# Four-block network on one core: the last layer norms start during the last attention group, the shared expert comes before the routed ones, and the end goes in four blocks

## The chip, the cores and the metric

One core of one Trainium2 chip. The metric is the device time of the kernel in microseconds (us); lower is better.

## The reference

2048 tokens of 128 numbers pass four sub-blocks, each of the form `x = x + norm(f(norm(x)))`: linear attention, a feed-forward with low-rank experts, causal attention that keeps the 64 largest scores of a row, and a second feed-forward. Only the last one and the norms around it matter here:

```python
x = x + _layernorm(_L1_attn_ref(_layernorm(x, axis=-1), ...), axis=-1)
x = x + _layernorm(_L1_ffn_ref(_layernorm(x, axis=-1), ...), axis=-1)
...
normed = _layernorm(hidden_states, ln_w, ln_b)
xf = normed.reshape(-1, h)
logits = xf @ router_w
top_idx = jnp.argmax(logits, axis=-1)
top_score = jax.nn.sigmoid(jnp.max(logits, axis=-1))
w = jnp.where(top_idx == e, top_score, 0.0)[:, None]      # for each expert e of 8
xe = xf * w
hmid = jax.nn.silu(xe @ g) * (xe @ u)
routed = routed + hmid @ d
shared = jax.nn.silu(xf @ sh_gate) * (xf @ sh_up) @ sh_down
moe_out = (routed + shared)
return hidden_states + moe_out
```

So between the attention and the router stand three norms: that of the attention's output, that before the feed-forward, and the feed-forward's own with a weight and an offset (`ln_w`, `ln_b`). The feed-forward's input is added to its output before the last norm.

## The kernel before, in words

The 2048 tokens are 16 tiles of 128 rows; a tile lies on the 128 partitions. The third sub-block runs in 64 groups k of four heads, four groups for each tile (tile t is groups 4t to 4t+3). The scores of group k stand in slot k mod 3 of a ring `S` in the large buffer `R`; each slot has 8256 numbers a partition. `SA` and `BIG` are names of parts of `R`: `SA` starts at slot 0, `BIG` at slot 2, and behind slot 2 lie the two scratch rows `A`.

The engines work in program order and meet at semaphores. Around the last group (k = 63, NG = 64) the order of each is this:

- VectorE (`dve`): pivots, MAX8 searches and `threshold` for each group; the last thing of a group is four masks (L1263). Then `memory_weights(63)` (L1353) and `weigh_heads` of groups 62 and 63 (L1259), a wait for the last accumulation `s_acc`, and the norms over all 16 tiles: `normalize` (L1019) does 16 `bn_stats`, 16 `bn_aggr`, an addition of epsilon, waits for ScalarE's square root, a reciprocal and 16 scalings. Norm, residual into `X`, norm, norm, two affine passes over all tiles (L1374, L1375).
- ScalarE (`act`): `exponent` of the four heads (L614), the copy `drain_heads(62)` (L597), then one drain for each of the 16 turned blocks of the group (`drain_turn`, L621), `drain_rest`, `drain_heads(63)`. Only then `sqrt(6)`, `sqrt(7)`, `sqrt(8)` (L471). A change to a function of another table puts an ACT_TABLE_LOAD ahead of it.
- TensorE (`pe`): in `values(k)` for each block j a turn (L890, L891: transposition of four score blocks with the mask) into one of two PSUM banks, then the product with the values (L906). Turn j+1 is issued ahead of product j; a turn waits until the drain of the bank two turns earlier is done, product j for drain j. `outputs(63)` closes the group (L924, L927).
- GpSimd (`pool`): four additions for the heads of each group (L442 to L451) after `rden`; the last one adds to `ACC` and raises `s_acc`.
- SyncE (`sp`): reload of `X` (L370) when the last MAX8 is done (`s_eight`), then `ln_w`, `ln_b` and six weight loads (L373 to L380) when group 63 is turned, then the output as one transfer (L382).

The second feed-forward starts when the normed rows `N1` are written (`s_rows` 4). TensorE turns all four blocks of four tiles (L963), computes the router's logits for 16 tiles (L969) and waits; VectorE finds the expert (`first_max`), ScalarE makes the sigmoid, VectorE multiplies the rows by the score (L1383, `s_rows` 5), TensorE turns those (L975). Then come 36 rounds, one for each expert e and block b of 512 tokens, e = 0 to 7 routed and e = 8 (`E0`) shared: `up(n)` makes gate and up (L986), ScalarE applies silu to the gate (L670), VectorE multiplies (`hidden`, L1397), `down(n)` (L994), and VectorE adds into `Y` (`gather`, L1411 for a routed expert, L1407 for the shared one). `plan_ffn1` lists the PSUM fills in order with the engine that drains each; fill n goes into bank n mod 8 after fill n-8 is drained. The up of round n+1 is issued ahead of the down of round n:

```python
up(0)
for n in range(4 * (E0 + 1)):
    if n + 1 < 4 * (E0 + 1):
        up(n + 1)
    down(n)
```

After the last round VectorE norms all 16 tiles, adds to `X` (L1425), and SyncE writes the 1 MB.

## Time and profile before

| | us |
|---|---|
| median of 3 runs (2819.96 to 2825.53) | 2820.38 |
| profiled execution, its own time | 2827.31 |
| span of the profiled execution | 2825.4 |
| TensorE matmuls busy in it | 2227.3 (79%) |
| VectorE busy in it | 2221.3 (79%) |
| ScalarE busy in it | 1570.8 (56%) |
| GpSimd busy in it | 563.0 (20%) |

The span is the time between the first and the last thing recorded on the core; its own time has 1.9 us around it. Shares of busy time are means over stages of very different kind. In the rows, PE is TensorE, DVE VectorE, ACT ScalarE, POOL GpSimd and SP SyncE; an engine's name with a q is its instruction queue, L with a number a line of the kernel, and a bracket at the end of a row gives the idle time before it and what ended that. Granted clock 1.00 is 2.4 GHz and 0.50 is 1.2 GHz; a value between them is a stretch with both.

### The profile page before, as it was taken

To read this page: it belongs to the slowest core of one execution; us is meant where nothing else is said; L and a number is where in the kernel's file an instruction comes from. 1 tells how busy PE (TensorE), PEld (TensorE's weight loads), DVE (VectorE), ACT (ScalarE), POOL (GpSimd) and SP (SyncE) were. 2 spreads that over 40 slices of the span, in tenths; PEclk is the share of its full clock that TensorE was granted. 3 is DMA by queue.
4 is the path that set the end of the run, shared out by engine and by line. 5 is a ranking of instruction groups with operands and counts; after the bars stand their busy time and mean duration, and the time that the engine had idled before them with its cause. 6 is when DMAs were issued, how large, how long until landed. Compare 5 with 4: busy or idle time off the path is not lost.

```text
span 2825.4 us, 34844 instructions
## 1 busy us (share of the span) xinstructions
PE 2227.3 (79%) x10182; PEld 1302.3 (46%) x10182; DVE 2221.3 (79%) x8987; ACT 1570.8 (56%) x2335; POOL 563.0 (20%) x427
## 2 busy tenths in 40 slices
PE   6599546677787668888888888898957888973997
PEld 2555333334444334455444445455434444542664
DVE  2504599999999989999999999888888878755445
ACT  1121234555666557777777777777737767661221
POOL 0000012222223222232222223223111312320000
PEclk7699667778989889999999999999978999986999
DMA  2000000000000000000000000000000000001000
GB/s 64 1 1 1 15 1 1 1 1 1 1 1 1 0 1 1 1 1 1 1 1 1 1 1 1 1 1 1 1 0 1 1 1 1 1 16 53 1 1 15
DMA packets 18021, 13.65 MB, mean 5 GB/s; under 512 B 6924, under 2 KB 15766, under 8 KB 17814
## 3 DMA queue, kind: packets, MB, share of 16 engines
q1 hardware_dynamic: 13776, 8.92, 1.2%
q10 hardware_dynamic: 4038, 2.37, 0.3%
q8 instruction: 81, 1.33, 0.2%
q14 instruction: 126, 1.03, 0.1%
HBM read 9.19 MB, written 2.10 MB: 4 GB/s over the span
## 4 chain that ended last, share of the span: by engine, by line
PE 45%; DVE 30%; ACT 17%; issue 6%; DVEq 2%; ACTq 1%; POOL 0%; POOLq 0%
PE bank L906 11%; PE bank L874 9%; DVE cand L1190 8%; ACT signs L591 5%; PE bank L890 5%; PE bank L986 4%; ACT R L614 3%; ACT R L564 3%; DVE W L1222 3%; DVE W L1221 3%; PE bank L891 3%; ACT R L607 2%; DVE F L1263 2%; PE bank L994 2%; PE bank L790 1%
## 5 line engine op out<-in xcount | busy, mean ns | idle before, releaser
L906 PE MATMUL bank<-WP,Y 128*128 128x512 f32 x1088 | 645.6, 679 | 168.0 <-ACT WP L621 166.2
L874 PE MATMUL bank<-hT,qT 128*128 128x512 f32 (+3 forms) x1280 | 564.9, 578 | 144.2 <-ACT R L564 96.2
L1190 DVE MAX8 cand<-R 128x8 f32<-128x12 f32 (+15 forms) x4096 | 666.9, 221 | 7.9 <-ACT R L564 7.4
L431 POOL TENSOR_TENSOR X<-R,X 128x144 f32<-128x144 f32 (+15 forms) x64 | 164.3, 2568 | 1934.0 <-ACT X L607 1934.0
L621 ACT ACTIVATE WP<-bank 128x512 f32<-128x512 f32 x544 | 320.9, 593 | 259.3 <-PE bank L891 249.0
L890 PE MATMUL bank<-ident,R 128*128 128x128 f32 x2176 | 446.2, 288 | 14.9 <-ACT R L614 14.9
L874 PEld LDWEIGHTS bank<-hT,qT 128*128 128x128 f32 x1280 | 237.7, 205 | 392.4 <-issue 185.9
L891 PE MATMUL bank<-nidentb,F 128*128 128x128 bf16 x2176 | 416.0, 226 | 0.0
L890 PEld LDWEIGHTS bank<-ident,R 128*128 128x128 f32 x2176 | 320.2, 147 | 154.6 <-issue 110.6
L564 ACT ACTIVATE R<-bank 128x1024 f32<-128x1024 f32 (+7 forms) x384 | 290.3, 773 | 156.5 <-PE bank L874 92.7
L614 ACT ACTIVATE R<-R,negm 128x144 f32<-128x144 f32 (+15 forms) x256 | 309.9, 1213 | 100.3 <-DVEq L1347 100.3
L591 ACT ACTIVATE signs<-R,cutb 128x144 int8<-128x144 f32 (+15 forms) x256 | 309.1, 1207 | 1.6
L891 PEld LDWEIGHTS bank<-nidentb,F 128*128 128x128 bf16 x2176 | 230.5, 106 | 132.5 <-issue 132.5
L906 PEld LDWEIGHTS bank<-WP,Y 128*128 128x128 f32 x1088 | 178.0, 206 | 227.1 <-ACT WP L621 220.5
L1263 DVE TENSOR_SCALAR F<-R,thr 128x144 bf16<-128x144 f32 (+15 forms) x256 | 197.0, 771 | 78.8 <-PE bank L891 77.3
L1250 DVE SCALAR_TENSOR_TENSOR R<-R,r 128x144 f32<-128x144 f32 (+15 forms) x128 | 235.7, 1841 | 4.5
L431 POOL TENSOR_TENSOR R<-R 128x144 f32<-128x144 f32 (+15 forms) x64 | 228.3, 3567 | 0.0
L1222 DVE TENSOR_TENSOR W<-W 128x256 f16<-128x256 f16 x768 | 216.8, 282 | 0.0
L1221 DVE TENSOR_TENSOR W<-W 128x256 f16<-128x256 f16 x768 | 207.9, 271 | 0.4
L1252 DVE MAX8 r<-R 128x8 f32<-128x144 f32 (+15 forms) x128 | 167.9, 1311 | 4.4
L607 ACT ACTIVATE X<-R,cutb 128x144 f32<-128x144 f32 (+15 forms) x64 | 77.5, 1212 | 137.6 <-DVE cutb L1236 137.6
L670 ACT ACTIVATE R<-bank 128x512 f32<-128x512 f32 x76 | 45.4, 597 | 146.6 <-PE bank L986 138.3
(239 smaller groups left out, 2720.3 us busy)
## 6 DMA issues: line engine op xcount, KB each, us to landing
out<-X SPq DMA_DIRECT2D x2, 1024.0 KB, 5.1
R<-in_L_attn_Wkv ACTq DMA_DIRECT2D x2, 512.0 KB, 8.4
R<-in_L_ffn_gate_w SPq DMA_DIRECT2D x1, 1024.0 KB, 6.4
R<-in_L_ffn_up_w SPq DMA_DIRECT2D x1, 1024.0 KB, 9.4
R<-in_L_attn_Wq ACTq DMA_DIRECT2D x1, 512.0 KB, 6.5
WP<-in_L_attn_Wo ACTq DMA_DIRECT2D x1, 512.0 KB, 11.1
R<-in_L_ffn_wi SPq DMA_DIRECT2D x1, 256.0 KB
R<-in_L_ffn_wo SPq DMA_DIRECT2D x1, 256.0 KB
```

Source lines behind the costliest of these rows:

```text
L431: pool.tensor_tensor(OV[i - 2][:, 0:n], S[:, k % NS, i, 0:n], OV[i - 2][:, 0:n], ALU.subtract)\
L564: act.activation(S[:, k % NS, i, MEM + SC * c:MEM + SC * c + w], src[:, 0:w], ACT.Copy)\
L591: act.activation(signs[:, 0:n], S[:, k % NS, i, 0:n], ACT.Sign, bias=cutb[:, k % 2, i:i + 1], scale=BIG_, accum_out=cnt[:, k % 2, i:i + 1] ...
L614: act.activation(row, row, ACT.Exp, bias=negm[:, k % 2, i:i + 1], scale=1.0 / LOW).then_inc(s_prob, 1)
L621: act.activation(PT[:, b % 4, :], bank[4 + n % 2], ACT.Relu).then_inc(s_tdrain, 1)
L874: last = pe.matmul(to, qT[:, k % 2, i, :], hT[:, a:b], start=True, stop=b < n, skip_group_check=True)
L890: pe.transpose(to[:, P * i:P * i + P], S[:, k % NS, i, blk], ident[:, :])
L891: last = pe.matmul(to[:, P * i:P * i + P], F[:, i, blk], nidentb[:, :], start=False, stop=True, skip_group_check=True)
L906: pe.matmul(bank[6], Y[:, j, :], PT[:, (blocks_before(k) + j) % 4, :], start=(j == 0), stop=(j == k // 4))\
L1190: mark(dve.max(cand[:, :, c, i], lists(S[:, k % NS, i, 0:n], n, c)))
L1221: mark(dve.tensor_tensor(dst[:, :, 0, :], src[:, :, 0, :], src[:, :, 1, :], ALU.max))
L1222: step = beside(step, dve.tensor_tensor(dst[:, :, 1, :], src[:, :, 0, :], src[:, :, 1, :], ALU.min))
```

## The change

- The three norms, the residual and the affine pass are split into tiles 0 to 14 (`front`) and tile 15 (`back`). VectorE does the front ones right after the last `threshold`, with `memory_weights(63)` and `weigh_heads(62)` after the first norm, and `weigh_heads(63)` only after the front's affine pass. The back ones follow when GpSimd's last accumulation is done.
- ScalarE's square roots for the front stand in the last group: the first after `drain_heads(62)` and ahead of the first turn's drain, the second ahead of turn 8's, the third ahead of turn 13's.
- The buffers of the last stage move: weights to slot 2 (group 62), `N1` and `lnw` to slot 1 (group 61), the copy `X2` of the normed input into the scratch rows `A`, `sg` and `hm` to slot 0. So the loads of `lnw` wait for group 61, those of the weights for group 62.
- The 36 rounds begin with the shared expert. Up of round 0 needs only tiles 0 to 3, so it goes ahead of the logits; tile 15's block is turned after the logits of tiles 0 to 11. The routing, the sigmoid, the scaled rows and their transposition stand between the shared expert's rounds.
- The last norm, the residual and the output go in four blocks of four tiles. Statistics of a block follow its last `gather`; blocks 0 and 1 are written after the statistics of block 2 and before the last `gather`.

```diff
@@ -140,30 +140,41 @@
+def ffn1_order():
+
+    return [(e, b) for e in (E0, *range(E0)) for b in range(4)]
+
+
...
+    for b in range(3):
+        f.add(("xf", b), "act")
     up(0)
-    for n in range(4 * (E0 + 1)):
-        if n + 1 < 4 * (E0 + 1):
+    f.add(("xf", 3), "act")
+    f.add("logit1", "dve")
+    for n in range(len(order)):
+        if n + 1 < len(order):
             up(n + 1)
-        f.add(("d", *divmod(n, 4)), "dve")
+        if n == 3:
+            f.add(("d", *order[3]), "dve")
+            continue
+        f.add(("d", *order[n]), "dve")
+        if n == 2:
+            for b in range(4):
+                f.add(("xs", b), "act")
...
@@ -274,15 +285,16 @@
-        gw_sb = SA[:, 0:2304].rearrange("p (e i) -> p e i", e=E0 + 1)
-        uw_sb = SA[:, 2304:4608].rearrange("p (e i) -> p e i", e=E0 + 1)
-        dw_sb = SA[:, 4608:6912].rearrange("p (e i d) -> p e i d", e=E0 + 1, i=2)
-        N1 = SA[:, 6912:8960].rearrange("p (t c) -> p t c", t=NT)
-        xsT = SA[:, 11008:13056]
-        lnw = SA[:, 13056:13312].rearrange("p (a c) -> p a c", a=2)
-        sg = BIG[:, 0:2048].rearrange("p (r c) -> p r c", r=4)
-        hm = BIG[:, 2048:6144].rearrange("p (r i c) -> p r i c", r=4, i=2)
-        XS = BIG[:, 6144:8192].rearrange("p (t c) -> p t c", t=NT)
+        gw_sb = BIG[:, 0:2304].rearrange("p (e i) -> p e i", e=E0 + 1)
+        uw_sb = BIG[:, 2304:4608].rearrange("p (e i) -> p e i", e=E0 + 1)
+        dw_sb = BIG[:, 4608:6912].rearrange("p (e i d) -> p e i d", e=E0 + 1, i=2)
+        X2 = BIG[:, 8256:10304].rearrange("p (t c) -> p t c", t=NT)
+        N1 = SA[:, 8256:10304].rearrange("p (t c) -> p t c", t=NT)
+        lnw = SA[:, 10304:10560].rearrange("p (a c) -> p a c", a=2)
+        xsT = SA[:, 10560:12608]
+        XS = SA[:, 12608:14656].rearrange("p (t c) -> p t c", t=NT)
+        sg = SA[:, 0:2048].rearrange("p (r c) -> p r c", r=4)
+        hm = SA[:, 2048:6144].rearrange("p (r i c) -> p r i c", r=4, i=2)
...
             sp.wait_ge(s_park, 16)
+            sp.wait_ge(s_tfill, turned(NG - 3))
+            sp.wait_ge(s_pm, NG - 2)
+            sp.dma_start(lnw[:, 0, :], ln_w.rearrange("(a n) -> a n", a=1).to_broadcast([P, P])).then_inc(s_ln, 16)
+            sp.dma_start(lnw[:, 1, :], ln_b.rearrange("(a n) -> a n", a=1).to_broadcast([P, P])).then_inc(s_ln, 16)
             sp.wait_ge(s_eight, UNITS)
             sp.dma_start(X[:, :, :], out[0].rearrange("(t p) c -> p t c", p=P)).then_inc(s_x, 16)
-            sp.wait_ge(s_tfill, turned(NG - 1))
-            sp.wait_ge(s_pm, NG)
-            sp.dma_start(lnw[:, 0, :], ln_w.rearrange("(a n) -> a n", a=1).to_broadcast([P, P])).then_inc(s_ln, 16)
-            sp.dma_start(lnw[:, 1, :], ln_b.rearrange("(a n) -> a n", a=1).to_broadcast([P, P])).then_inc(s_ln, 16)
+            sp.wait_ge(s_tfill, turned(NG - 2))
+            sp.wait_ge(s_pm, NG - 1)
...
-            sp.wait_ge(s_y1, 1)
-            sp.dma_start(out[0].rearrange("(t p) c -> p t c", p=P), X[:, :, :]).then_inc(s_out, 16)
-            sp.wait_ge(s_out, 16)
+            for b in range(4):
+                sp.wait_ge(s_y1, b + 1)
+                sp.dma_start(out[0, 512 * b:512 * b + 512, :].rearrange("(t p) c -> p t c", p=P), X[:, 4 * b:4 * b + 4, :])\
+                    .then_inc(s_out, 16)
+            sp.wait_ge(s_out, 64)
...
-            def sqrt(n):
+            def sqrt(n, first=0, last=NT):
                 act.wait_ge(s_var, n)
-                act.activation(std[:, :], mv[:, :, 1], ACT.Sqrt).then_inc(s_std, 1)
+                act.activation(std[:, first:last], mv[:, first:last, 1], ACT.Sqrt).then_inc(s_std, 1)
...
                         drain_heads(p - 2)
+                    if p == NG:
+                        sqrt(6, 0, NT - 1)
                     for j in turns[0:3]:
...
                 if p >= 1:
                     for j in turns[7 if p < NG else 3:]:
+                        if p == NG and j in (8, 13):
+                            sqrt(7 if j == 8 else 8, 0, NT - 1)
                         drain_turn(p - 1, j)
...
-            sqrt(6)
-            sqrt(7)
-            sqrt(8)
-            for b in range(4):
+            for b in range(3):
                 fdrain(("xf", b), hT[:, 512 * b:512 * b + 512])
+            for n in (9, 10, 11):
+                sqrt(n, NT - 1, NT)
+
+            def gate(n):
+                for i in range(2):
+                    k = 2 * n + i
+                    if k >= 4:
+                        m = (k - 4) // 2
+                        act.wait_ge(s_fdrain_v, ffills.drained(ffills.index(("u", *order[m], k % 2))))
+                    fdrain(("g", *order[n], i), sg[:, k % 4, :], ACT.Silu)
+
+            gate(0)
+            fdrain(("xf", 3), hT[:, 1536:2048])
+            gate(1)
             act.wait_ge(s_sig_in, 1)
             act.activation(sm[:, 5, :], sm[:, 4, :], ACT.Sigmoid).then_inc(s_sig, 1)
+            gate(2)
+            gate(3)
             for b in range(4):
                 fdrain(("xs", b), xsT[:, 512 * b:512 * b + 512])
-            for e in range(E0 + 1):
-                for b in range(4):
-                    for i in range(2):
-                        k = (e * 4 + b) * 2 + i
-                        if k >= 4:
-                            m = (k - 4) // 2
-                            act.wait_ge(s_fdrain_v, ffills.drained(ffills.index(("u", *divmod(m, 4), k % 2))))
-                        fdrain(("g", e, b, i), sg[:, k % 4, :], ACT.Silu)
-            sqrt(9)
+            for n in range(4, len(order)):
+                gate(n)
+            for b in range(4):
+                sqrt(12 + b, 4 * b, 4 * b + 4)
...
-            pe.wait_ge(s_rows, 4)
-            for b in range(4):
...
-            pe.wait_ge(s_fdrain_a, 4)
-            pe.wait_ge(s_ln, 48)
-            k = open_ffill("logit1")
-            for t in range(NT):
-                last = pe.matmul(k[:, E0 * t:E0 * t + E0], hT[:, P * t:P * t + P], rw_sb[:, :], start=True, stop=True)
-            last.then_inc(s_ffill, 1)
-            pe.wait_ge(s_rows, 5)
-            for b in range(4):
-                k = open_ffill(("xs", b))
-                for i in range(4):
-                    last = pe.transpose(k[:, P * i:P * i + P], XS[:, 4 * b + i, :], ident[:, :])
-                last.then_inc(s_ffill, 1)
-            pe.wait_ge(s_fdrain_a, 8)
-            pe.wait_ge(s_wf, 16 * 6)
 
             def up(n):
-                e, b = divmod(n, 4)
+                e, b = order[n]
+                if e == 0:
+                    pe.wait_ge(s_fdrain_a, ffills.drained(ffills.index(("xs", b))))
                 src = (xsT if e < E0 else hT[:, :])[:, 512 * b:512 * b + 512]
...
+            pe.wait_ge(s_rows, 4)
+            for b in range(3):
+                turn_xf(b)
+            pe.wait_ge(s_fdrain_a, 3)
+            pe.wait_ge(s_wf, 16 * 6)
             up(0)
-            for n in range(4 * (E0 + 1)):
-                if n + 1 < 4 * (E0 + 1):
+            pe.wait_ge(s_ln, 48)
+            logit = open_ffill("logit1")
+            for t in range(12):
+                pe.matmul(logit[:, E0 * t:E0 * t + E0], hT[:, P * t:P * t + P], rw_sb[:, :], start=True, stop=True)
+            pe.wait_ge(s_rows, 5)
+            turn_xf(3)
+            pe.wait_ge(s_fdrain_a, ffills.drained(ffills.index(("xf", 3))))
+            for t in range(12, NT):
+                last = pe.matmul(logit[:, E0 * t:E0 * t + E0], hT[:, P * t:P * t + P], rw_sb[:, :], start=True, stop=True)
+            last.then_inc(s_ffill, 1)
+            for n in range(len(order)):
+                if n + 1 < len(order):
                     up(n + 1)
                 down(n)
+                if n == 2:
+                    for b in range(4):
+                        pe.wait_ge(s_rows, 6 + b)
+                        k = open_ffill(("xs", b))
+                        for i in range(4):
+                            last = pe.transpose(k[:, P * i:P * i + P], XS[:, 4 * b + i, :], ident[:, :])
+                        last.then_inc(s_ffill, 1)
...
-            def normalize(src, dst):
-
-                norms[0] += 1
-                for t in range(NT):
+            def spread(src, first=0, last=NT):
+                for t in range(first, last):
                     mark(dve.bn_stats(st6[:, t, :], src[:, t, :]))
                 dve.wait_ge(s_dve, done[0])
-                for t in range(NT):
+                for t in range(first, last):
                     mark(dve.bn_aggr(mv[:, t, :], st6[:, t, :]))
                 dve.wait_ge(s_dve, done[0])
-                dve.tensor_scalar(mv[:, :, 1], mv[:, :, 1], EPS, None, ALU.add).then_inc(s_var, 1)
-                dve.wait_ge(s_std, norms[0])
-                link(dve.reciprocal(rstd[:, :], std[:, :]))
-                for t in range(NT):
+                dve.tensor_scalar(mv[:, first:last, 1], mv[:, first:last, 1], EPS, None, ALU.add).then_inc(s_var, 1)
+                norms[0] += 1
+                return norms[0]
+
+            def scaled(src, dst, norm, first=0, last=NT):
+                dve.wait_ge(s_std, norm)
+                link(dve.reciprocal(rstd[:, first:last], std[:, first:last]))
+                for t in range(first, last):
                     mark(dve.tensor_scalar(dst[:, t, :], src[:, t, :], mv[:, t, 0:1], rstd[:, t:t + 1],
                                            ALU.subtract, ALU.mult))
                 dve.wait_ge(s_dve, done[0])
+
+            def normalize(src, dst, first=0, last=NT):
+                scaled(src, dst, spread(src, first, last), first, last)
...
+            def affine(first, last):
+
+                rows_ = N1[:, first:last, :]
+                link(dve.tensor_tensor(rows_, rows_, lnw[:, 0, :].unsqueeze(1).to_broadcast([P, last - first, P]), ALU.mult))
+                dve.tensor_tensor(rows_, rows_, lnw[:, 1, :].unsqueeze(1).to_broadcast([P, last - first, P]), ALU.add)\
+                    .then_inc(s_rows, 1)
+
+            def residual(first, last):
+                link(dve.tensor_tensor(X[:, first:last, :], X[:, first:last, :], N1[:, first:last, :], ALU.add))
+
+            front, back = (0, NT - 1), (NT - 1, NT)
+            dve.wait_ge(s_acc, NG - 4)
+            dve.wait_ge(s_tfill, turned(NG - 3))
+            normalize(ACC, N1, *front)
             memory_weights(NG - 1)
-            for k in (NG - 2, NG - 1):
-                weigh_heads(k)
+            weigh_heads(NG - 2)
+            dve.wait_ge(s_x, 32)
+            residual(*front)
+            normalize(X, X2, *front)
+            normalize(X2, N1, *front)
+            dve.wait_ge(s_ln, 48)
+            affine(*front)
+            weigh_heads(NG - 1)
             dve.wait_ge(s_acc, NG)
-
-
-            normalize(ACC, N1)
-            dve.wait_ge(s_x, 32)
-            link(dve.tensor_tensor(X[:, :, :], X[:, :, :], N1, ALU.add))
-            normalize(X, Y)
-            normalize(Y, N1)
-            dve.wait_ge(s_ln, 48)
-            link(dve.tensor_tensor(N1, N1, lnw[:, 0, :].unsqueeze(1).to_broadcast([P, NT, P]), ALU.mult))
-            dve.tensor_tensor(N1, N1, lnw[:, 1, :].unsqueeze(1).to_broadcast([P, NT, P]), ALU.add).then_inc(s_rows, 1)
-            n = ffills.index("logit1")
-            dve.wait_ge(s_ffill, n + 1)
-            dve.tensor_copy(L.rearrange("p t e -> p (t e)"), bank[n % 8][:, 0:NT * E0]).then_inc(s_fdrain_v, 1)
-            dve.wait_ge(s_fdrain_v, 1)
-            first_max(L, sm[:, 4, :], oh1)
-            dve.sem_inc(s_sig_in, 1)
-            dve.wait_ge(s_sig, 1)
-            dve.tensor_tensor(XS, N1, bc(sm[:, 5, :], P), ALU.mult).then_inc(s_rows, 1)
+            normalize(ACC, N1, *back)
+            residual(*back)
+            normalize(X, X2, *back)
+            normalize(X2, N1, *back)
+            affine(*back)
...
             hidden(0)
-            for n in range(4 * (E0 + 1)):
-                if n + 1 < 4 * (E0 + 1):
+            k = ff("logit1")
+            dve.tensor_copy(L.rearrange("p t e -> p (t e)"), k[:, 0:NT * E0]).then_inc(s_fdrain_v, 1)
+            dve.wait_ge(s_fdrain_v, ffills.drained(ffills.index("logit1")))
+            first_max(L, sm[:, 4, :], oh1)
+            dve.sem_inc(s_sig_in, 1)
+            hidden(1)
+            gather(0)
+            dve.wait_ge(s_sig, 1)
+            for b in range(4):
+                dve.tensor_tensor(XS[:, 4 * b:4 * b + 4, :], N1[:, 4 * b:4 * b + 4, :], bc(sm[:, 5, 4 * b:4 * b + 4], P), ALU.mult)\
+                    .then_inc(s_rows, 1)
+            last = len(order) - 4
+            norm = [0] * 4
+
+            def settled(b):
+
+                dve.wait_ge(s_dve, done[0])
+                dve.wait_ge(s_fdrain_v, ffills.drained(ffills.index(("d", *order[last + b]))))
+                norm[b] = spread(X2, 4 * b, 4 * b + 4)
+
+            def written(b):
+                scaled(X2, N1, norm[b], 4 * b, 4 * b + 4)
+                dve.tensor_tensor(X[:, 4 * b:4 * b + 4, :], X[:, 4 * b:4 * b + 4, :], N1[:, 4 * b:4 * b + 4, :], ALU.add)\
+                    .then_inc(s_y1, 1)
+
+            for n in range(1, len(order)):
+                if n + 1 < len(order):
                     hidden(n + 1)
                 gather(n)
-            dve.wait_ge(s_dve, done[0])
-            dve.wait_ge(s_fdrain_v, ffills.engine.count("dve"))
-            normalize(Y, N1)
-            dve.tensor_tensor(X[:, :, :], X[:, :, :], N1, ALU.add).then_inc(s_y1, 1)
+                if n >= last:
+                    settled(n - last)
+                if n == last + 2:
+                    written(0)
+                    written(1)
+            written(2)
+            written(3)
```

## Rows read from the trace of the kernel before

**Rows 1.** The page's strip of 40 slices: granted clock in tenths.

```profile
PEclk7699667778989889999999999999978999986999
```

**Rows 2.** The chain of waits from the last group on: start us, us, what.

```profile
2564.20 0.46 POOL WP L451
...
2599.87 3.69 PE bank L963 x16
...
2604.23 3.90 PE bank L969 x32
...
2617.11 9.22 PE bank L986 x16
...
2626.33 1.78 PE bank L994 x16
...
2628.11 3.44 PE bank L986 x8
...
2803.81 3.58 PE bank L994 x32
```

**Rows 3.** Stretches: bounds, us, busy by engine, granted clock, DMA share, GB/s.

```profile
2523.00:2561.00 38.00, 31.26 (x171) 18.90 (x171) 0.55 (x3) 18.82 (x24) 2.66 (x4) 0.87 0.05 15
...
2626.00:2807.00 181.00, 181.00 (x848) 115.79 (x847) 85.53 (x200) 41.98 (x70) 0.00 (x0) 1.00 0.00 1
```

**Rows 4.** Short stretches of TensorE in and after the last group: the same, PE only.

```profile
2534.00:2536.00 2.00, 2.00 (x10) 0.50 0.00 0
...
2536.00:2538.00 2.00, 2.00 (x12) 1.00 0.00 0
...
2562.00:2564.00 2.00, 0.00 (x0) 0.83 1.06 327
```

**Rows 5.** VectorE's timeline: start us, us, line, operation, operands, count.

```profile
2521.87 1.27 DVE L1263 TENSOR_SCALAR F<-R,thr 128x2064 bf16<-128x2064 f32 x1
...
2561.43 0.18 DVE L1259 RECIPROCAL rden<-Zs 128x4 f32<-128x4 f32 x1 [29.77 <-ACT Zs L597]
...
2564.68 3.19 DVE L1023 BATCH_NORM_STATS2 st<-WP 128x6 f32<-128x128 f32 x16 [3.07 <-POOL WP L451]
...
2567.91 1.17 DVE L1026 BATCH_NORM_AGGREGATE mv<-st 128x2 f32<-128x6 f32 x16
...
2569.86 4.19 DVE L1032 TENSOR_SCALAR R<-WP,mv,rstd 128x128 f32<-128x128 f32 x16
...
2574.08 2.29 DVE L1370 TENSOR_TENSOR X<-X,R 128x2048 f32<-128x2048 f32 x1
...
2608.80 0.29 DVE L1098 TENSOR_TENSOR cand<-cand,sm 128x128 f32<-128x128 f32 x1
...
2628.15 1.13 DVE L1411 SCALAR_TENSOR_TENSOR Y<-bank,cand,Y 128x128 f32<-128x128 f32 x4 [1.03 <-PE bank L994]
...
2817.61 2.29 DVE L1425 TENSOR_TENSOR X<-X,R 128x2048 f32<-128x2048 f32 x1
```

**Rows 6.** ScalarE's timeline: the first square root and its table; the last group.

```profile
14.12 1.28 ACT L471 ACT_TABLE_LOAD   x1 [14.12 <-issue]
...
15.41 0.22 ACT L471 ACTIVATE std<-mv 128x16 f32<-128x16 f32 x1
...
2530.88 0.57 ACT L597 ACTIVATE Zs<-bank 128x512 f32<-128x512 f32 x1
...
2552.01 0.60 ACT L621 ACTIVATE WP<-bank 128x512 f32<-128x512 f32 x1 [0.99 <-PE bank L891]
```

**Rows 7.** SyncE's timeline (reload, first and last weight load); DMA issues, size, us to landing.

```profile
2506.73 0.71 SPq L370 DMA_DIRECT2D X<-out  x1
...
2557.64 0.43 SPq L375 DMA_DIRECT2D R<-in_L_ffn_gate_w  x1
...
2567.77 0.43 SPq L380 DMA_DIRECT2D R<-in_L_ffn_sh_down  x1
...
out<-X SPq DMA_DIRECT2D x2, 1024.0 KB, 5.1
...
R<-in_L_ffn_sh_down SPq DMA_DIRECT2D x1, 128.0 KB, 4.4
...
R<-in_L_ffn_ln_w SPq DMA_DIRECT2D x1, 64.0 KB, 2.9
```

34 lines of the change are left out of this document (15 added, 19 removed).

## The prediction

> **What bounds the kernel now.** I read the strip of the page first, then the chain of waits from the end backwards, then the stretches with their granted clock, and last the timelines of VectorE and ScalarE around the last group. The strip shows an average only; the granted clock in it moves between 6 and 9 tenths in the loop [rows 1]. The change touches nothing before the last group (k=63), so only the last 300 us count. There the chain has three parts. GpSimd finishes the last accumulation at 2564.66 (2564.20 + 0.46) and VectorE takes over; TensorE gets its first work of the second feed-forward at 2599.87 [rows 2]. In these 35.2 us TensorE has nothing to do: three layer norms, a residual and the affine pass run on VectorE in a row. Then transposes, router logits, routing, scaled rows and more transposes alternate until the expert matmuls start at 2617.11 [rows 2]. From 2626 to 2807 TensorE is busy 181.00 of 181.00 us at granted clock 1.00 [rows 3]: a round costs 3.44 (up, L986 x8) + 1.78 (down, L994 x16) = 5.22 us, and the matmuls end at 2803.81 + 3.58 = 2807.39 [rows 2]. VectorE's norm and the 1 MB output close the span at 2825.4. Before that, in the last group (2523 to 2561), VectorE is busy 0.55 us of 38 [rows 3]: that is the cover the change moves the norms under.
>
> **Part 1: norms of tiles 0 to 14 beside the last group.** VectorE ends its last mask at 2523.14 [rows 5]. What the norms wait for is there: the sum for tile 14 was finished four groups ago, group 61's slot was turned before group 62's, X's reload is issued at 2506.73 [rows 7]. Prices from the 16-tile norm [rows 5]: stats 3.19, aggregation 1.17, from its end (2569.08) to the first scaling (2569.86) 0.78 for epsilon, square root and reciprocal, scaling 4.19, each pass of 2048 elements 2.29. For 15 tiles: 3.0, 1.1, 0.8, 3.95, 2.15. The first variance is ready at about 2527.5, but the square root sits in ScalarE's queue behind the exponents and the copy of the heads, which ends at 2531.45 [rows 6]. There it also loads a table: 1.28 us, and the square root follows at once (14.12 + 1.28, next start 15.41) [rows 6]. So std is there at 2532.95; scaling ends 2537.2; Pm and rden (0.2 each) 2537.65; residual 2539.9; second variance 2544.3. ScalarE asks for it before turn 8, near 2545.8, so it does not wait; std 2546.0, scaling to 2550.3, third variance 2554.7. It is asked for before turn 13: turn 12's drain began at 2552.01 [rows 6], so with the shift below ScalarE comes at 2553.7 and stands for 1.0 us. The next drain is 0.3 late, and a turn plus a product of PE lie between; I cost that at nothing (0 to 1 us). Scaling ends 2559.2, two affine passes 2563.6.
>
> What it costs: the load and the first square root hold up ScalarE's drain of turn 0 by 1.5 us. TensorE still has turn 1 to do, so product 0 starts 1.1 us later. The clock is low there anyway (0.50 at 2534, 1.00 from 2536) [rows 4]; if its rise comes later too, each microsecond at the low level costs half. I take +1.6, between +1.1 and +4.
>
> Moved past others: Pm goes 6.5 us later, needed by TensorE only at the end of the group; the heads of group 62 likewise go to GpSimd 6.2 us later, and its four operations (3.2 us with the reciprocal, [rows 5] 2561.43 to [rows 2] 2564.66) are asked for 20 us later. Weights: six loads now go out when group 62 is turned (2518). In the trace their issue runs from 2557.64 to 2568.2 and the last lands 4.4 us after its issue, 15 us in all [rows 7]; so 2533, with over 30 us spare. lnw goes ahead of X's reload in SP's queue: 0.8 us of issue, while SP waits for VectorE anyway.
>
> The group ends 1.6 us later, so the heads of group 63 are copied at 2563.0, and VectorE turns to them after the affine pass, at 2563.6. GpSimd ends at 2566.9. Tile 15 then passes alone through the same steps. With 0.29 for an operation of 128 elements [rows 5], 0.2 for stats and 0.15 to 0.25 for the tiny ones, a norm is about 1.3; three, a residual and two affine passes 4.8: 2571.7.
>
> A rule against this part: two engines at one port. No row shows a residual pass beside GpSimd's additions. The bound from the rows is the whole head chain, 3.2 us on the front chain, and nothing at the other end. I take nothing, because VectorE issues the residual before GpSimd's multiplication can start. The Trainium skill (SBUF — State Buffer, on the shared port pair) says that a VectorE operation with two inputs in SBUF and a GpSimd operation reading SBUF exclude one another, whoever starts first; by that GpSimd would wait, and the sum stays.
>
> **Part 2: the shared expert first.** TensorE turns 12 tiles from 2563.6. 16 transposes took 3.69 at the low clock [rows 2], so 2.8, or 1.4 at the high one. The clock was still 0.83 in the 2 us after 2562 although the engine had stopped at 2561 [rows 4], so a mix: 2565.9. Drain 0.65: 2566.6. Up(0): 3.44 at the high clock, 6.9 at the low one; the first 16 took 9.22 against 6.88 [rows 2]; I take 5.2: 2571.8. Logits of 12 tiles at 3.90/16 each: 2.9, 2574.7. Tile 15 is there. Four transposes 0.6, drain 0.7, four logits 1.0: 2577.0. ScalarE is ready for that drain at about 2573.5 (last square root 2570.4, table 1.3, two gates). From there 35 ups and 36 downs and 16 transposes at the high clock (1.85): 120.4 + 64.1 + 1.85 = 186.3, so TensorE ends at **2763.3** instead of 2807.4: **-44.1**. Routing (copy and five steps of 0.3), sigmoid with two table loads (2.8) and the scaled rows (2.3) now lie beside up and down of blocks 0 to 2, 15.7 us of TensorE, in which VectorE's own work is 6.2. I cost them at nothing; without that cover they are 7 on the path.
>
> **Part 3: the end in blocks.** After TensorE's end VectorE has: gather(34) done at +0.6 (four operations 1.13 [rows 5]), settled(2) 1.2 (4 x 0.20, 4 x 0.07, the rest), written(0) and written(1) 1.9 each (4 x 0.26 + 0.57 + reciprocal), gather(35) 1.1, settled(3) 1.3, written(2) and (3) 1.9 each: +10.9. Before it was 2819.9 - 2807.4 = +12.5 [rows 5]. The last transfer is 256 KB: between 2.9 (64 KB) and 5.1 (1 MB) [rows 7], by the line between them 3.35, with issue 3.7 instead of 5.5. Tail 14.6 instead of 18.0: **-3.4**.
>
> Sum: 2825.4 - 44.1 - 3.4 = 2777.9 of span, -47.5. The profiled execution took 2827.3, so 2779.8 by its own measure. It is 6.9 above the median of the runs, 2820.4; that surplus lies in parts the change leaves alone. Against the median: **2772.9**.
>
> **The rivals.**
> (a) ScalarE's queue stalls the last group. Square roots 2 and 3 wait for VectorE inside the turn loop. For it: the third is asked for a microsecond early. If VectorE runs late, drains stop, TensorE starves and its clock falls, as it did around the exponents (2534: 0.50) [rows 4]. The 25 us from 2536 to 2561 would then take up to 25 more: up to 2798. Against it: drains wait for TensorE, not the reverse, and one late drain is absorbed. 8%.
> (b) A table switch costs more than its load. If each switch took twice the load, 1.28 more, product 0 and the front chain would go 1.3 later, and the two loads around the sigmoid would still fit: 2774.2. Against it: no such gap behind the load [rows 6]. 5%. The Trainium skill (ScalarE: Activation LUTs, What ACT_TABLE_LOAD costs) gives 1283 ns plus a drain of about 1380 ns for a switch to another set; the load agrees with this trace, the drain does not show in it.
> (c) The norms do not move: something VectorE waits for comes only with the last group. Then only part 3 and the routing remain, -3.4 - 13 (2612 to 2599 hidden) = 2804; with the shared rounds held up too, 2817. Every semaphore named above was reached before 2532, so 3%.
> (d) Slower than before: the 39 us rest of TensorE before the experts is gone, and the stage of 190 us is granted the low clock instead of 1.00 [rows 3]. At half speed it costs 190 more: 2963. It decides from a mean granted clock below 0.80 (190/0.80 - 190 = 47.5). For it: the loop shows slices at 6 to 7 tenths [rows 1]. Against it: the clock was low after TensorE had stood still (2523 to 2534) and full where it was fed [rows 4]; the new stage feeds it. 3%.
> The forecast has 81%.
>
> **How the numbers follow.** Low end: a full clock throughout part 2 (-2.8), +1.1 in the last group (-0.5) and 3 us of the spread between runs: 2766. High end: the late clock (+2.4), the port (+3.2), (b) and a full transfer time (+1.7): 2782, which also holds the mild half of (a). No change within 0.2% (5.6 us, about what a measurement tells) needs most of (c): 2%. Slower: (d), 3%. Faster: 95%.
>
> **What would show it.** Right: stats of ACC right behind the last mask at 2523; a table load in the last group with the square root directly behind; the group's last product 1 to 2 us later; TensorE's first transposes at 2563 to 2565; 5.22 per round from the second on; four output transfers. Wrong: ScalarE waiting at the square roots before turns 8 or 13 for over a microsecond, a granted clock below 1.00 after 2580, TensorE waiting at the logits of tile 15 for ScalarE's gates, or the last transfer landing 5 us after issue.

## The result, and the profile after

The changed kernel takes 2777.18 us (median of 4 runs, 2774.97 to 2783.13) against 2822.95 for the kernel before on the same chip: a ratio of 0.9837 (95% interval 0.982 to 0.9854), 45.8 us less. The forecast was 2772.9, 47.5 less than before. In a later series the same kernel gave 0.9841 (0.982 to 0.9863).

The work ahead of the last group is the same in both kernels, but for the time of some loads, and still differs by a few us from one execution to the next. So two profiles are best compared by the **last stage**: from the start of group 63's exponents to the end of the span. Before: 2825.4 - 2523.24 = 302.2. After: 2781.0 - 2527.07 = 253.9. Difference 48.2; the forecast's sum was 47.5. A second profile of the changed kernel (e13 below) gives 255.6, so a difference of 46.5. All times with a plus sign below count from the start of those exponents.

ScalarE's timeline after: start us, us, line, operation, operands, count, idle before and what ended it.

```profile
2527.07 7.73 ACT L630 ACTIVATE R<-R,negm 128x2064 f32<-128x2064 f32 x4 [2.77 <-DVEq L1389]
2534.71 0.57 ACT L613 ACTIVATE Zs<-bank 128x512 f32<-128x512 f32 x1
2535.30 1.28 ACT L487 ACT_TABLE_LOAD   x1
2536.60 0.21 ACT L487 ACTIVATE std<-mv 128x15 f32<-128x15 f32 x1
...
2549.52 0.21 ACT L487 ACTIVATE std<-mv 128x15 f32<-128x15 f32 x1
...
2558.40 0.22 ACT L487 ACTIVATE std<-mv 128x15 f32<-128x15 f32 x1 [0.82 <-DVE mv L1063]
...
2565.78 0.60 ACT L613 ACTIVATE Zs<-bank 128x512 f32<-128x512 f32 x1 [1.54 <-PE bank L955]
...
2574.79 1.28 ACT L690 ACT_TABLE_LOAD   x1
2576.09 1.08 ACT L690 ACTIVATE R<-bank 128x512 f32<-128x512 f32 x2
2577.06 0.60 ACT L690 ACTIVATE hT<-bank 128x512 f32<-128x512 f32 x1
```

The first square root follows its table load at once, at +9.5; [rows 6] had the same 1.28 and the same missing gap. The second waits for nobody, the third 0.82 us for VectorE. The copy of group 63's heads starts at +38.7; before it started at 2560.81, +37.6. That 1.1 is less than the roots cost the last group, because the two profiles differ in where TensorE's clock falls. In the kernel before, the low level (granted clock 0.50) lasts 10.2 us in this group, from +2.5 to +12.8. In this profile it lasts 13.6, from +0.5 to +14.2. Profiles in which it begins at the same place differ by 2.1: +36.6 (e3, which has no roots there) against +38.7 here, both from +0.5, and +37.6 against +39.7 (e1, e7, e8), all from +2.5. So the roots cost the group 2.1, of which 1.7 is the low level that lasts 3.4 us longer.

VectorE's timeline after, same columns:

```profile
2525.71 1.27 DVE L1305 TENSOR_SCALAR F<-R,thr 128x2064 bf16<-128x2064 f32 x1
2527.19 3.00 DVE L1058 BATCH_NORM_STATS2 st<-WP 128x6 f32<-128x128 f32 x15 [0.21 <-DVE F L1305]
...
2536.84 0.25 DVE L1069 RECIPROCAL rstd<-std 128x15 f32<-128x15 f32 x1 [5.31 <-ACT std L487]
...
2541.33 2.13 DVE L1412 TENSOR_TENSOR X<-X,R 128x1920 f32<-128x1920 f32 x1
...
2549.76 0.25 DVE L1069 RECIPROCAL rstd<-std 128x15 f32<-128x15 f32 x1 [1.93 <-ACT std L487]
...
2565.10 2.16 DVE L1408 TENSOR_TENSOR R<-R 128x1920 f32<-128x1920 f32 x1
2567.18 0.17 DVE L1301 RECIPROCAL rden<-Zs 128x4 f32<-128x4 f32 x1
2570.42 0.29 DVE L1058 BATCH_NORM_STATS2 st<-WP 128x6 f32<-128x128 f32 x1 [3.07 <-POOL WP L467]
...
2575.71 0.29 DVE L1408 TENSOR_TENSOR R<-R 128x128 f32<-128x128 f32 x1
```

This answers to [rows 5]: the statistics of the attention's output begin 0.2 us behind the last mask, not 41 us behind it. The front chain ends at 2567.26, +40.2, and the group's last product at 2565.75: the norms of 15 tiles lay under the group except for 1.5 us. VectorE itself stands 5.31 us for the first root and 1.93 for the second, which is behind the drains in ScalarE's queue, so the chain moves with the turns. Tile 15 alone takes from 2570.42 to 2576.00.

TensorE's timeline after, and its stretches (bounds, us, busy, granted clock, DMA share, GB/s):

```profile
2564.59 1.16 PE L955 MATMUL bank<-M,Zs 128*128 128x128 f32 x8
2567.32 1.53 PE L990 MATMUL bank<-ident,R 128*128 128x128 f32 x12 [1.57 <-DVE R L1408]
2569.64 3.70 PE L1001 MATMUL bank<-hT,R 128*128 128x512 f32 x8 [0.79 <-ACT hT L690]
...
2576.06 0.66 PE L990 MATMUL bank<-ident,R 128*128 128x128 f32 x4
2577.72 1.06 PE L1027 MATMUL bank<-rw_sb,hT 128*128 128x8 f32 x8 [1.00 <-ACT hT L690]
```

```profile
2542.00:2565.00 23.00, 23.00 (x138) 1.00 0.01 1
2566.00:2578.00 12.00, 8.75 (x51) 1.00 0.00 1
2578.00:2583.00 5.00, 5.00 (x14) 0.66 0.00 0
2583.00:2766.80 183.80, 183.80 (x867) 1.00 0.00 1
```

From 2542 on the clock is full, and the second feed-forward starts at the high clock, where before it started at the low one [rows 2]. Right behind the last logits the clock falls once more: 0.66 in the 5 us from 2578, which is 3.4 us at the low level. After that a round is again 5.22 us, and TensorE is busy without a gap to 2766.82, +239.7, against 2807.37, +284.1, before.

The end, VectorE's timeline and the DMA issues (size, us to landing):

```profile
2765.05 1.13 DVE L1459 SCALAR_TENSOR_TENSOR R<-bank,cand,R 128x128 f32<-128x128 f32 x4 [1.03 <-PE bank L1009]
...
2767.89 1.11 DVE L1071 TENSOR_SCALAR R<-R,mv,rstd 128x128 f32<-128x128 f32 x4
...
2771.61 1.12 DVE L1459 SCALAR_TENSOR_TENSOR R<-bank,cand,R 128x128 f32<-128x128 f32 x4
...
2777.55 0.69 DVE L1488 TENSOR_TENSOR X<-X,R 128x512 f32<-128x512 f32 x1
```

```profile
out<-X SPq DMA_DIRECT2D x4, 256.0 KB, 2.3
```

### The profile page after: what moved, and what is told of

Read it like the earlier page. It is cut to its first block, busy times and chain, and to the rows that moved or that the text cites. A ratio compares the mean times of both kernels' runs of the same rounds, so it can differ in the third digit from the quotient of the medians.

```text
span 2781.0 us, 34886 instructions
## 1 busy us (share of the span) xinstructions
PE 2232.8 (80%) x10182; PEld 1304.3 (47%) x10182; DVE 2228.3 (80%) x9008; ACT 1572.2 (57%) x2342; POOL 565.0 (20%) x427
## 3 DMA queue, kind: packets, MB, share of 16 engines
q14 instruction: 126, 1.03, 0.1%
## 4 chain that ended last, share of the span: by engine, by line
PE 42%; DVE 34%; ACT 16%; issue 6%; DVEq 2%; ACTq 1%; POOL 0%; POOLq 0%
PE bank L934 10%; DVE cand L1232 10%; PE bank L902 8%; ACT signs L607 5%; PE bank L918 5%; PE bank L1001 4%; ACT R L630 3%; DVE W L1264 3%; DVE W L1263 3%; DVE F L1305 3%; ACT R L580 3%; PE bank L919 2%; ACT R L623 2%; PE bank L1009 2%; DVE R L1292 1%
## 5 line engine op out<-in xcount | busy, mean ns | idle before, releaser
L447 POOL TENSOR_TENSOR X<-R,X 128x144 f32<-128x144 f32 (+15 forms) x64 | 162.7, 2542 | 1937.6 <-ACT X L623 1937.6
## 6 DMA issues: line engine op xcount, KB each, us to landing
out<-X SPq DMA_DIRECT2D x4, 256.0 KB, 2.3
WP<-in_L_attn_Wo ACTq DMA_DIRECT2D x1, 512.0 KB, 11.2
R<-in_L_ffn_wi SPq DMA_DIRECT2D x1, 256.0 KB
```

The costliest lines, as they stand in the source:

```text
L447: pool.tensor_tensor(OV[i - 2][:, 0:n], S[:, k % NS, i, 0:n], OV[i - 2][:, 0:n], ALU.subtract)\
```

## The experiments

Two measures stand beside each other for each kernel: the last stage, and in it TensorE's last matmul and the tail behind it. The changed kernel has two profiles of its own (first, and once more in the last series). "Low clock" is the time at the low level in the first 75 us of the stage, summed over slices of 1 us as 2 x (1 - granted clock).

| kernel | last stage | last matmul | tail | low clock |
|---|---|---|---|---|
| before | 302.2 | +284.1 | 18.0 | 45.2 |
| changed, first | 253.9 | +239.7 | 14.2 | 17.0 |
| changed, again (e13) | 255.6 | +241.5 | 14.2 | 20.5 |
| e1 end in one block | 260.2 | +241.7 | 18.5 | 20.5 |
| e2 shared expert last | 261.5 | +248.2 | 13.3 | 27.3 |
| e3 norms after the group | 291.1 | +277.0 | 14.2 | 47.2 |
| e4 second table load | 256.3 | +242.2 | 14.2 | 20.5 |
| e5 late norms | 259.3 | +245.1 | 14.2 | 20.5 |
| e6 roots moved | 257.7 | +243.6 | 14.1 | 23.9 |
| e7 up(1) first | 255.5 | +241.3 | 14.2 | 20.5 |
| e8 additions on GpSimd | 256.1 | +241.7 | 14.4 | 20.5 |
| e10 fed at the last logits | 256.0 | +241.8 | 14.2 | 20.5 |
| e11 roots moved, fed | 255.6 | +241.4 | 14.2 | 17.1 |
| e12 heads between passes | 258.4 | +244.3 | 14.2 | 23.9 |

**e13, the changed kernel again.** No edit.

> The changed kernel itself once more, for the spread: whether the dip of TensorE's clock behind the last logits is 2 us long, as in its first profile, or 4, as in four experiments with the same order there. Either theory of the dip: ratio to the kernel before 0.982 to 0.986, last stage between 253.9 and 256.5.

Ratio 0.9841 (0.982 to 0.9863), last stage 255.6. Same code, 1.7 us more, all of it ahead of the last matmul. It comes in two parts. The first transposes start at +41.06 instead of +40.25: the low level in the last group is as long as in the first profile (13.6) but begins and ends 1.7 later, the turns with it, and ScalarE reaches the second root at +23.3 instead of +22.5. The other 0.9 comes behind: the clock falls at +50.0, while tile 15's transposes run, and stays low for 6.8 us instead of 3.4. So one profile can't tell changes under 2 us here unless they show as their own lines. It helps to compare profiles in which the group's low level begins at the same place: at +0.5 in the first profile, e3 and e6, at +2.2 to +2.5 in all others.

**e1, undo part 3.**

```diff
-                if n >= last:
-                    settled(n - last)
-                if n == last + 2:
-                    written(0)
-                    written(1)
-            written(2)
-            written(3)
+            normalize(X2, N1)
+            dve.tensor_tensor(X[:, :, :], X[:, :, :], N1, ALU.add).then_inc(s_y1, 1)
```

> The changed kernel with its end in one piece again: one norm over 16 tiles after the last gather, one output transfer of 1 MB. Measured by the last stage, from the start of the last group's exponents to the end of the span: 302.2 us in the kernel before, 253.9 in the changed one. My theory: the blocks earn what part 3 of the sum says, so 257.3 (+3.4). Rival: gather(35) stands behind written(0) and written(1) on VectorE, so the blocks earn only the shorter transfer: 255.7 (+1.8) or less.

Tail 18.5 against 14.2: the blocks earn 4.3, the rest of the stage's 6.3 (or 4.6 against e13) lies ahead of the last matmul, in the part that e1 leaves alone. The rival falls. The tail is also 0.5 longer than the 18.0 of the kernel before, which ends in the same one piece: the last `gather` is now a routed expert's (1.13) and was the shared one's (0.69). Ratio 0.984 (0.9818 to 0.9862); in whole runs 4 us drown.

**e2, undo part 2.**

```diff
-    return [(e, b) for e in (E0, *range(E0)) for b in range(4)]
+    return [(e, b) for e in range(E0 + 1) for b in range(4)]
```

and logits, routing, sigmoid, rows and transposes ahead of `up(0)` on all engines.

> The changed kernel with the shared expert last again: all logits, routing, sigmoid, scaled rows and their transposition come before the first round; early norms and block-wise end stay. My theory: logits, routing, two table loads, scaled rows and transposes come back on the path, +11 to +14 on the last stage (253.9 in the changed kernel), and TensorE's clock is low when the first round starts. Rival: the routing chain was short enough to hide behind tile 15's norms, +5 or less.

Stage +7.6 against the first profile, +5.9 against e13; ratio 0.9849 (0.9829 to 0.9869). Both expectations missed; mine by more. Its TensorE, which starts its first round at 2580.37:

```profile
2570.20 1.11 PE L981 MATMUL bank<-ident,R 128*128 128x128 f32 x4 [3.57 <-DVE R L1398]
...
2576.90 3.68 PE L1022 MATMUL bank<-ident,R 128*128 128x128 f32 x16 [3.03 <-DVE R L1462]
2580.37 7.16 PE L992 MATMUL bank<-R 128*128 128x512 f32 x16
```

The two waits are 3.57 for tile 15's rows and 3.03 for routing, sigmoid and scaled rows. The logits and the transposes themselves are TensorE's own work in either order; I had counted them as coming back. The prediction had said 7 for the routing chain, and that stands. The last matmul comes 6.7 us later than in e13, and the tail takes 0.9 back (13.3), because here the last two `gather`s are the shared expert's.

**e3, undo part 1.**

```diff
-            normalize(ACC, N1, *front)
             memory_weights(NG - 1)
             weigh_heads(NG - 2)
+            weigh_heads(NG - 1)
+            dve.wait_ge(s_acc, NG)
+            normalize(ACC, N1)
```

and so on for all 16 tiles, the three square roots behind `drain_heads(63)`.

> The changed kernel with its three norms over all 16 tiles after the last accumulation again; shared expert first and block-wise end stay. My theory: the front chain was hidden almost whole, so TensorE's first transposes come 36 us later, less the 3 us that it now stands at tile 15's logits: +33 to +36 on the last stage (253.9). Rival: the norms cost the last group more than 2 us, so undoing them costs only 30 or less, and the group's last product comes over 2 us earlier than in the changed kernel.

Stage +37.2 (+35.5 against e13), ratio 0.996 (0.9947 to 0.9973). So the early norms carry three quarters of the gain, and the other two parts alone earn 0.4% of the run. The rival's number (30 or less) falls, though its sign shows: the group's heads are copied at 2558.98 - 2522.39 = +36.6, 2.1 earlier than in the first profile of the changed kernel. In both the group's low level begins at +0.5, so 37.2 and 2.1 are the fair numbers, and 37.2 lies 1.2 above my range. The kernel before has e3's order there and copies the heads at +37.6, with a low level that is as long but begins 2.0 later.

The three parts together: 35.5 to 37.2, 5.9 to 7.6 and 4.3 make 45.7 to 49.1, against 48.2 (e13: 46.5) between before and after. Nothing large is left unexplained.

**e4, a second table load.**

```diff
                     if p == NG:
+                        act.activation(std[:, NT - 1:NT], std[:, NT - 1:NT], ACT.Silu)
                         sqrt(6, 0, NT - 1)
```

> The changed kernel with one tiny silu activation ahead of the first square root in the last group, so that two table loads stand there instead of one. My theory: a switch costs its load and nothing more, 1.28 plus 0.2 for the activation: the last stage goes from 253.9 to 255.4, and each activation starts within 0.05 us of its load's end. Rival (b): a switch costs about twice its load, and the stage grows by 2.8.

ScalarE's timeline of this kernel:

```profile
2530.39 1.28 ACT L664 ACT_TABLE_LOAD   x1
2531.68 0.20 ACT L664 ACTIVATE std<-std 128x1 f32<-128x1 f32 x1
2531.89 1.28 ACT L487 ACT_TABLE_LOAD   x1
2533.18 0.21 ACT L487 ACTIVATE std<-mv 128x15 f32<-128x15 f32 x1
```

Each function starts 0.01 behind its load, with other work directly ahead of both loads: a switch costs 1.28 here and nothing besides. The root comes 1.5 later (+11.0 against +9.5). The stage is 2.4 longer than in the first profile and 0.7 longer than e13; my 1.5 lies between the two. Rival (b) falls by the rows, though the stage alone could not have told.

**e5, VectorE late on purpose.**

```diff
             residual(*front)
+            for again in range(2):
+                for t in range(NT - 1):
+                    mark(dve.bn_stats(st6[:, t, :], X[:, t, :]))
+                dve.wait_ge(s_dve, done[0])
             normalize(X, X2, *front)
```

> The changed kernel with two more passes of 15 statistics (6.0 us of VectorE, results overwritten) between the residual and the second norm of tiles 0 to 14, so that ScalarE must wait at the square roots inside the turn loop. The second root had 1.9 us to spare. My theory: ScalarE stands 4 us ahead of turn 8, TensorE runs out of turns for about 3, and the last stage grows by the lateness of VectorE's chain alone: 253.9 to 258 (+4), up to 260 if TensorE's clock dips once more. Rival (a): the stall takes the clock away for the rest of the group, 8 turns at half speed, and the group's last product comes over 10 us later: 264 or more.

ScalarE's timeline and TensorE's stretch:

```profile
2552.73 0.22 ACT L487 ACTIVATE std<-mv 128x15 f32<-128x15 f32 x1 [3.49 <-DVE mv L1063]
...
2561.62 0.22 ACT L487 ACTIVATE std<-mv 128x15 f32<-128x15 f32 x1 [2.52 <-DVE mv L1063]
```

```profile
2549.00:2567.00 18.00, 15.58 (x87) 1.00 0.00 1
```

ScalarE stands 3.49 and 2.52 us inside the turn loop, TensorE is short of 2.4 us of work in 18, and its granted clock stays 1.00. The stage grows by 5.3, or by 3.6 against e13, whose low level in the group begins at the same place; VectorE's front chain ends at +44.6 against e13's +41.0, which is the same 3.6. Rival (a) needs more than this: in this profile late roots cost their lateness, not the clock.

**e6, roots one step later.**

```diff
                     for j in turns[0:3]:
                         drain_turn(p - 1, j)
+                        if p == NG and j == 1:
+                            sqrt(6, 0, NT - 1)
...
-                        if p == NG and j in (8, 13):
+                        if p == NG and j in (9, 14):
```

> The changed kernel with its three early square roots one step later in ScalarE's queue: the first behind the drain of turn 1 instead of ahead of turn 0, the others ahead of turns 9 and 14. ScalarE idled 3 us there. My theory: product 0 starts 1.1 us earlier and the group ends 1.1 earlier, but VectorE's chain (affine pass of tiles 0 to 14) sets the start of what follows, so the last stage gains nothing but clock: 253.9, within 1.5. Rival: the delay of the turns was on the path, and the stage falls by 1.1 or more with VectorE's last affine pass at the same place.

The group does end earlier: heads at 2563.35 - 2526.56 = +36.8 instead of +38.7, and the group's low level lasts 10.2 us instead of 13.6. VectorE's affine pass ends at +40.6 instead of +40.2. And the kernel is slower, 257.7. Its TensorE:

```profile
2567.23 2.11 PE L990 MATMUL bank<-ident,R 128*128 128x128 f32 x12 [3.92 <-DVE R L1408]
2570.03 6.08 PE L1001 MATMUL bank<-hT,R 128*128 128x512 f32 x8 [0.69 <-ACT hT L690]
```

```profile
2564.00:2567.00 3.00, 0.00 (x0) 1.00 0.00 0
2567.00:2576.00 9.00, 8.08 (x22) 0.62 0.00 0
```

It stands 3.92 us, the clock is still 1.00 while it stands, then it falls: `up(0)` takes 6.08 instead of 3.70 and the transposes 2.11 instead of 1.53. My "nothing but clock, within 1.5" was wrong by the clock.

**e11, the same with TensorE fed.**

```diff
+            for spare in range(4):
+                pe.matmul(bank[1], ident[:, :], hT[:, 0:512], start=True, stop=True)
             pe.wait_ge(s_rows, 4)
```

and one more such matmul ahead of the wait for tile 15's drain.

> The kernel with the roots moved one step later, with four spare 512-column matmuls behind the group's last product, where TensorE stood 3.9 us before the first transposes, and the one spare matmul ahead of the last logits. With the roots moved the last stage was 257.7, 3.8 more than in the changed kernel, though VectorE's chain ended at the same place. My theory: TensorE's clock fell in the longer standstill and that is the whole loss, so with it fed the stage is 252.5 to 254. Rival: the loss has another cause, and the stage stays over 256.

```profile
2560.13 3.60 PE L1014 MATMUL bank<-hT,ident 128*128 128x512 f32 x8
...
2565.88 3.70 PE L1001 MATMUL bank<-hT,R 128*128 128x512 f32 x8 [0.79 <-ACT hT L690]
```

(Each fp32 matmul stands as two in the rows.) `up(0)` is back at 3.70, the first transposes still start at +40.7, and the stage is at 255.6, e13's value. Both forecasts miss, mine of 252.5 to 254 and the rival's of over 256. That e6 lost `up(0)`'s 2.4 us to the clock is shown, since the spare matmuls do no work that anything needs. They bring no gain over the changed kernel, though, because the dip behind the logits stays (0.53 from 2575 to 2580). It begins at +50.0, although TensorE had been fed from the group's end on, busy 11.73 of the 12.67 us before.

**e10, one spare matmul ahead of the last logits.** The second edit of e11 alone.

> The changed kernel with one spare 512-column matmul, result unused, between tile 15's transposes and the logits that wait for their drain. TensorE stood 1.0 us there and its clock dipped right after, for 2 to 4 us in the runs so far. Last stage of the changed kernel: 253.9 with a short dip, 256.1 in the run with the additions on GpSimd, which had the same order up to there and a long one. My theory: the standstill brings the dip, so feeding it keeps the clock at 1.00: 252.5 to 253.5. Rival: the dip comes from the light work around it (logits, transposes), or from elsewhere, and the stage stays at 254 to 256.

```profile
2569.80:2581.00 11.20, 10.26 (x51) 0.90 0.01 1
2582.00:2586.00 4.00, 4.00 (x9) 0.56 0.00 0
```

Busy 10.26 of 11.2 us instead of 8.75 of 12, and the dip is as long as in e13, 6.8 us: 256.0, ratio 0.9851 (0.9831 to 0.987). The order in time says more than the length: here and in e13 the clock falls at +50.0, while tile 15's transposes run, so ahead of the standstill that I fed. My theory of a dip by that standstill falls, and the stage is where the rival had put it. What brings it stays open; what precedes it in every profile of the changed order is a stretch of transposes and 8-column logits.

**e7, up(1) ahead of tile 15.**

```diff
             up(0)
+            up(1)
+            pe.wait_ge(s_rows, 5)
+            turn_xf(3)
             pe.wait_ge(s_ln, 48)
             logit = open_ffill("logit1")
```

> The changed kernel with up(1) ahead of tile 15's transposes and of all logits (TensorE, its fill plan, ScalarE's and VectorE's order alike). In the changed kernel TensorE stands 2.5 us waiting for the drain of tile 15's rows behind three square roots and a table load, and its clock dips to 0.5 right after. My theory: that gap closes and the dip with it, -2 on the last stage (252). Rival: the wait only moves, since the drain now stands behind gate(1) as well: within 1 us of 253.9.

TensorE's timeline of this kernel:

```profile
2571.61 7.13 PE L1002 MATMUL bank<-hT,R 128*128 128x512 f32 x16 [0.79 <-ACT hT L691]
...
2584.33 3.76 PE L1010 MATMUL bank<-R 128*128 128x128 f32 x16
2587.88 3.96 PE L1002 MATMUL bank<-hT,R 128*128 128x512 f32 x8
```

255.5, 1.6 above the first profile and 0.1 below e13, and neither theory's mechanism. The wait is gone and did not move: from `up(0)` on TensorE stands 0.2 us in 23. (It had been 1.00 us in the changed kernel's rows, not the 2.5 of the text above.) The drain of tile 15's rows now stands behind four gates instead of two, but the 12 logits ahead of it cover that. The clock falls all the same (low clock 20.5), and now its low level lies over a `down` and part of an `up`, 3.76 instead of 1.95 and 3.96 instead of 3.60, where e13's lay over transposes, a wait, the last logits and part of `up(1)`.

**e8, the last additions on GpSimd; e12, the heads' reciprocal between the affine passes.**

```diff
+            for b in range(3):
+                pool.wait_ge(s_phi_in, 3 + b)
+                pool.tensor_tensor(X[:, 4 * b:4 * b + 4, :], X[:, 4 * b:4 * b + 4, :], N1[:, 4 * b:4 * b + 4, :], ALU.add)\
+                    .then_inc(s_y1, 1)
```

```diff
             link(dve.tensor_tensor(rows_, rows_, lnw[:, 0, :]..., ALU.mult))
+            weigh_heads(NG - 1)
             dve.tensor_tensor(rows_, rows_, lnw[:, 1, :]..., ALU.add).then_inc(s_rows, 1)
```

> The changed kernel with the last additions into X of blocks 0 to 2 on GpSimd instead of VectorE (3 x 0.69 us). VectorE is busy without a gap from TensorE's last matmul to its own end. My theory: VectorE bounds the end, so its end comes 2.0 earlier and the stage falls to 252. Rival: GpSimd's addition and VectorE's operations exclude one another, and VectorE gains less than 1; or block 2's transfer becomes the last to land.

> The changed kernel with the reciprocal for group 63's heads between VectorE's two affine passes instead of behind them. My theory: GpSimd starts up to 1.0 us earlier, tile 15's norms and with them the last logits too: -1 on the last stage, from 253.9 (256.1 with a long dip of the clock). Rival: the second affine pass, with two inputs in SBUF, and GpSimd's operations exclude one another, so GpSimd's four take 2 us longer or the pass does, and nothing is gained.

e8, both engines, then e12:

```profile
2772.49 1.26 POOL L472 TENSOR_TENSOR X<-X,R 128x512 f32<-128x512 f32 x1 [199.80 <-DVEq L1493]
2772.64 1.95 DVE L1075 TENSOR_SCALAR R<-R,mv,rstd 128x128 f32<-128x128 f32 x4
...
2779.13 1.89 DVE L1075 TENSOR_SCALAR R<-R,mv,rstd 128x128 f32<-128x128 f32 x4
```

```profile
2558.72 0.18 DVE L1301 RECIPROCAL rden<-Zs 128x4 f32<-128x4 f32 x1 [1.43 <-ACT Zs L613]
2558.82 2.13 DVE L1428 TENSOR_TENSOR R<-R 128x1920 f32<-128x1920 f32 x1
2559.05 2.79 POOL L458 TENSOR_TENSOR Zs<-Zs,rden 128x508 f32<-128x508 f32 x1 [21.44 <-DVE rden L1301]
```

In e8 the scaling of a block takes 1.12 alone and 1.95 and 1.89 beside GpSimd's addition, so VectorE ends 11.7 behind the last matmul instead of 11.4: 2.1 us of work moved, nothing gained. In e12 GpSimd's multiplication takes 2.79 beside the second affine pass; alone it takes 1.03, and the pass keeps its 2.13. So in these rows whoever starts first goes through and the other is held up. The Trainium skill (SBUF — State Buffer, Who interferes with whom) says that a VectorE instruction with two SBUF inputs contends with a GpSimd instruction that reads SBUF, and that issue order decides who blocks; e12's rows agree. For a scaling with one input, as in e8, it says so only in VectorE's two-port modes, and no row shows the mode.

The port is not all of e12's loss. Its stage is 258.4, 2.8 above e13, where I had forecast a gain of 1. The reciprocal needs ScalarE's copy of the heads, and VectorE stands 1.43 us for it between the two passes, so the second pass ends at +42.5 instead of e13's +41.0. TensorE therefore stood 3.01 us before the first transposes and started at the low clock, as in e6.

No kernel beat the changed one.

## Why the prediction was right, point by point

- **The front chain.** Forecast: root at 2532.95 (+9.7), affine pass done at 2563.6 (+40.4). Measured +9.7 (2536.81) and +40.2. The third root's wait was forecast as 1.0 and was 0.82; it delayed no turn visibly, since the drains keep their 1.59 rhythm.
- **The last group.** Forecast +1.6 between +1.1 and +4. Measured 2.1 between profiles whose low level begins at the same place. The mechanism is the forecast's: the drain of turn 0 comes later and the clock rises later, 3.4 us more at the low level, which costs 1.7.
- **Queues and loads.** The six weight loads went out from 2521.82; the last was issued at 2530.82 and landed 4.7 later, at 2535.5, 34 us ahead of its use. The cover held. The residual pass beside GpSimd took 2.13, as forecast from 2.15; it had started 0.22 ahead, and GpSimd's multiplication beside it took 2.79 instead of 1.03, at a place where nothing waits for it.
- **Tile 15.** Forecast 4.8, measured 5.6 (2570.42 to 2576.00): statistics of one tile are 0.29, not 0.2, and its scaling 0.35. I had taken sixteenths of a run of 16 for the statistics. That is 0.8 too little, and it cost almost nothing: TensorE's 12 logits end at 2575.92.
- **Up(0) and the clock.** Forecast: a mix of both clocks, 2.3 for the transposes and 5.2 for up(0). Measured 1.5 and 3.7, full clock throughout; that is 2.3 too much. From the front chain's end to `up(1)` it took 11.4 instead of 13.4. In its place the clock fell behind the logits, and up(1) took 5.2 instead of 3.44, 1.8 that I had not priced. The two errors cancel: TensorE's last matmul was forecast at +240.1 and came at +239.7 (e13: +241.5). The sum was right here partly by luck; e6 shows the other outcome, 2 to 4 us worse, and e12 has it in part.
- **The end.** Forecast 10.9 for VectorE and 3.7 for the output, measured 11.4 and 2.8 (the transfer of 256 KB lands after 2.3, below the lower end of 2.9 that I had). The 10.9 is also a wrong addition: its terms (0.6, 1.2, twice 1.9, 1.1, 1.3, twice 1.9) make 11.8, and with them the tail is 15.5 and the forecast 2773.8. Of the terms, gather(34) ends 0.6 ahead of the last matmul, not 0.6 behind it, and each `written` takes 2.0. Tail 14.2 against a forecast of 14.6; e1 gives 4.3 for the part, forecast 3.4.
- **The signs.** The signs of being right showed, with 5.22 per round from `up(2)` on. Of the signs of being wrong one showed, small: TensorE stood 1.00 us at the logits of tile 15, whose drain was behind a table load and two gates. The clock fell too, from +51.7 to +55.1, which is ahead of the 2580 (+56.8) that I had named.
- **The rivals.** (a) fell with e5: roots 4 us late stall ScalarE and leave the clock at 1.00. (b) fell with e4. (c) fell with the first lines of VectorE's timeline. (d) fell: granted clock 1.00 from 2583 to the last matmul, without the long rest before it.

## What to carry to other kernels

A serial chain on one engine, with all others idle, can often start before the loop in front of it ends: ask for each tile when its last input is written, not when the loop is done. Here 15 of 16 tiles were ready four groups early, and three quarters of the gain came from that. When helper instructions go into another engine's queue, look at which of the waits there already has slack; and when the path is set by one engine, ending another's work earlier may be worse than nothing, because it then stands and its clock falls.

## What the runs showed that I had not expected

- A group that ended 1.9 us earlier made the kernel 2 to 4 us slower (e6), and useless matmuls took 2 us of that back (e11).
- The clock falls once around or behind the logits in every order that had them between rounds, for 3.4 us (first profile, e12) or 6.8 us (all others), also with TensorE busy 11.73 of the 12.67 us ahead of it (e11).
- Where the low level of the last group begins differs between executions of the same kernel (+0.5 or +2.2), and with the square roots in ScalarE's queue this moves VectorE's chain too: 0.8 us of the 1.7 between the two profiles.
- An operation of 128 elements that stands alone costs 0.29 where its share in a row of such operations is 0.20 (statistics), 0.35 against 0.26 (scaling) and 0.18 against 0.07 (aggregation).
- GpSimd's multiplication of 508 elements a partition takes 2.79 instead of 1.03 beside a VectorE pass with two inputs in SBUF, and VectorE's scaling with one input takes 1.9 instead of 1.12 beside GpSimd's addition: moving work between these two engines is not free even where one is idle.
